# Half of a block's G groups behind its last layer-1 tile, and layer 2 dealt out over three periods, in a fused gather, interaction and tower kernel

## The reference

```
for W in (W0, W1):                       # W0: 39*39 x 128, W1: 39*128 x 128
    xk = einsum('bid,bjd,ijh->bhd', x0, xk, W.reshape(39, Hk, 128))
    outs.append(xk)
z = sum(concatenate(outs, axis=1), axis=-1)          # 512 x 256
h = relu(concatenate([z, dense_ctx]) @ W_top1 + b_top1)   # 272 -> 512
h = relu(h @ W_top2 + b_top2)                             # 512 -> 256
y = h @ W_top3                                            # 256 -> 1
```

## Time and profile before

| | us |
|---|---|
| median of three executions | 284.72 |
| the profiled execution | 284.26 |
| its span on the core | 282.5 |
| PE busy | 228.4 |
| DVE busy | 163.8 |
| ACT busy | 153.4 |
| POOL busy | 136.8 |

### The profile page before, as it was taken

The page is one execution under the profiler, slowest core; times in us unless marked ns, Lnnn a source line. Parts: engine busy times, 40 slices in busy tenths (PEclk is TensorE's granted clock), DMA queues, the critical chain, the costliest instruction groups (busy, mean ns, idle before and its releaser), DMA issues.

```text
span 282.5 us, 4480 instructions
## 1 busy us (share of the span) xinstructions
PE 228.4 (81%) x1548; PEld 190.5 (67%) x1548; DVE 163.8 (58%) x309; ACT 153.4 (54%) x298; POOL 136.8 (48%) x135
## 2 busy tenths in 40 slices
PE   0000349798988999984999999999999999999897
PEld 0000348455767777974977878999687799978696
DVE  6556660398875887535454786674566856542301
ACT  1133133599776897525384786654667857531301
POOL 4787777777777777777777777200000000000000
PEclk9999958669999999996899999999999999999999
DMA  4434640992210111111011012010101010000000
GB/s 78 112 121 123 169 128 9 251 284 33 28 29 10 26 23 21 29 19 19 6 17 22 9 26 31 7 24 3 23 2 17 8 25 9 15 15 12 2 0 0
DMA packets 29862, 12.58 MB, mean 45 GB/s; under 512 B 21438, under 2 KB 27672, under 8 KB 29840
## 3 DMA queue, kind: packets, MB, share of 16 engines
q1 hardware_dynamic: 25648, 11.22, 15.9%
q0 software_dynamic: 4192, 1.08, 4.6%
HBM read 9.66 MB, written 0.00 MB: 34 GB/s over the span
## 4 chain that ended last, share of the span: by engine, by line
PE 46%; POOL 34%; issue 13%; ACT 4%; DMA 2%; ACTq 0%
POOL emb L263 34%; PE turn_bank L340 10%; PE x_bank L305 5%; PE turn_bank L351 4%; PE x_bank L308 4%; PE x_bank L307 4%; PE pair_bank L288 4%; PE misc_bank L277 2%; PE turn_bank L374 2%; PE g_bank L328 2%; PE x_turn_bank L316 2%; PE g_bank L329 2%; PE g_bank L332 2%; ACT x1h L669 1%; ACT prod_hi L656 1%
## 5 line engine op out<-in xcount | busy, mean ns | idle before, releaser
L263 POOL DMA_INDIRECT emb<-tbl,ids_sb x131 | 136.6, 1043 | 42.1 <-issue 39.6
L651 ACT ACTIVATE prod<-pair_bank 128x512 f32<-128x512 f32 (+1 forms) x112 | 66.6, 598 | 46.9 <-PE pair_bank L288 46.9
L305 PE MATMUL x_bank<-prod_hi,pair_w_hi 128*128 128x512 f32 (+1 forms) x112 | 64.8, 579 | 4.5 <-ACT x1h L669 4.5
L531 DVE TENSOR_TENSOR prod_lo<-prod,prod_hi 128x512 fp32r<-128x512 f32 x96 | 62.1, 687 | 2.9
L288 PE MATMUL pair_bank<-x,sel 117*128 117x512 bf16 (+1 forms) x112 | 45.0, 407 | 7.8 <-ACT prod L651 6.2
L340 PE MATMUL turn_bank<-g_sb,w_sb 128*128 128x128 f32 x312 | 42.0, 277 | 0.6 <-ACT g_sb L684 0.6
L340 PEld LDWEIGHTS turn_bank<-g_sb,w_sb 128*128 128x128 f32 x312 | 40.2, 194 | 2.1 <-ACT g_sb L684 0.9
L656 ACT ACTIVATE prod_hi<-prod 128x512 fp32r<-128x512 f32 x64 | 40.3, 630 | 0.0
L308 PE MATMUL x_bank<-prod_hi,pair_w_lo 128*128 128x512 f32 x96 | 38.5, 401 | 0.0
L307 PE MATMUL x_bank<-prod_lo,pair_w_hi 128*128 128x512 f32 x96 | 38.3, 399 | 0.0
L521 DVE CAST prod_hi<-prod 128x512 fp32r<-128x512 f32 x48 | 21.5, 447 | 28.7 <-ACT prod L651 28.2
(11 more groups left out here) (92 smaller groups left out, 278.6 us busy)
## 6 DMA issues: line engine op xcount, KB each, us to landing
xblk<-xs SPq DMA_DIRECT2D x128, 20.0 KB
emb<-tbl,ids_sb POOLq DMA_INDIRECT x131, 2.5
tab<-small SPq DMA_DIRECT2D x2, 625.0 KB
wt<-w_top SPq DMA_DIRECT2D x2, 512.0 KB
small_ids_i<-small_ids SPq DMA_DIRECT2D x2, 500.0 KB
small_ids_i<-small_ids SPq DMA_DIRECT2D x1, 562.5 KB
tab<-small SPq DMA_DIRECT2D x1, 562.5 KB
wa<-pair_w_a SPq DMA_DIRECT2D x1, 448.0 KB, 14.8
```

The source lines that it names most:

```text
L263: pool.indirect_dma_start(out=emb[:, at:at + D], out_offset=None, in_=tables[f], in_offset=bass.IndirectOffsetOnAxis(ap=ids_sb[:, c * M + ...
L305: mm = pe.matmul(x1_bank[:, :], pair_w_hi[p, t, :], prod_hi[p, k % 2, t, :], start=(t == 0), stop=(t == FULL))
L531: dve.tensor_tensor(prod_lo[:, k % 2, t, :] if t < FULL else prod_hi[rows, k % 2, t, :], prod[rows, (NT * k + t) % RING, :], prod_hi[rows, ...
L651: act.activation(prod[0:ROWS[t], n % RING, :], pair_bank[n % 2][0:ROWS[t], :], ACT.Square).then_inc(sq_done, 1)
```

## The change

In each period PE issues groups 0 and 1 of `contract_d` at t = 4 and 5 and groups 2 and 3 behind the loop over t; before, the four stood at t = 3, 4, 5 and 6. The copies of G on ACT and DVE move accordingly. Layer 2 of a chunk, before 21 steps in the period with j = 2 and 18 in the one with j = 3, is dealt out evenly over 21 places in the periods with j = 2, j = 3 and the next j = 0 (13 steps in each), for chunk 2 over 14 places in two periods. The tower, before in the periods with j = 0 (`mlp1`, `mlp2`) and j = 1 (`mlp3`), stands wholly in the one with j = 1, and its last copy, `keep_y`, in the one with j = 2. The tail's code is the same.

```diff
+            def layer2_part(k, t):
+                c, j = k // NB, k % NB
+                at, n = {2: (c - 1, 0), 3: (c - 1, NT), 0: (c - 2, 2 * NT)}.get(j, (-1, 0))
+                steps = 2 * NT if at == NCH - 2 else 3 * NT
+                i0, i1 = ((n + t + e) * M // steps for e in (0, 1))
+                if 0 <= at and n + t < steps and i0 < i1:
+                    layer2(at, i0, i1)
...
@@ PE, period(k), for t in range(NT)
-                    if t >= NT - NG and k >= 2:
-                        contract_d(k - 2, t - (NT - NG))
-                    if j == 2 and c >= 1:
-                        layer2(c - 1, 3 * t, 3 * t + 3)
-                    if j == 3 and c >= 1 and t < 6:
-                        layer2(c - 1, 21 + 3 * t, 24 + 3 * t)
+                    if t in (4, 5) and k >= 2:
+                        contract_d(k - 2, t - 4)
+                    layer2_part(k, t)
...
-                    if j == 0 and c >= 2 and t == 2:
+                    if j == 1 and c >= 2 and t == 1:
                         mlp1(c - 2)
-                    if j == 0 and c >= 2 and t == 6:
+                    if j == 1 and c >= 2 and t == 4:
                         mlp2(c - 2)
-                    if j == 1 and c >= 2 and t == 1:
+                    if j == 1 and c >= 2 and t == 6:
                         mlp3(c - 2)
...
+                if k >= 2:
+                    contract_d(k - 2, 2)
+                    contract_d(k - 2, 3)
@@ DVE, period(k)
-                tiles(k, 4, 6)
-                if j == 0 and c >= 2:
+                if j == 1 and c >= 2:
                     relu1(c - 2)
+                tiles(k, 4, 7)
                 if k >= 2:
                     keep_g(k - 2, 1)
-                tiles(k, 6, NT + 1)
+                tiles(k, 7, NT + LAG)
                 if k >= 2:
                     keep_g(k - 2, 3)
-                tiles(k, NT + 1, NT + LAG)
@@ ACT, period(k)
+                if j == 1 and c >= 2:
+                    keep_z2(c - 2)
                 tiles(k, 0, 1)
                 if k >= 2:
                     keep_x1(k - 2)
...
-                if j == 0 and c >= 2:
-                    keep_z2(c - 2)
+                if j == 2 and c >= 2:
+                    keep_y(c - 2)
+                tiles(k, 1, 5)
+                if k >= 2:
+                    keep_g(k - 2, 0)
+                tiles(k, 5, 6)
...
                 if j == 1 and c >= 2:
                     relu2(c - 2)
-                tiles(k, 1, 4)
-                if k >= 2:
-                    keep_g(k - 2, 0)
-                if j == 1 and c >= 2:
-                    keep_y(c - 2)
-                tiles(k, 4, 6)
...
+                tiles(k, 6, 7)
+                keep_x1h(k - 1)
                 if k >= 2:
                     keep_g(k - 2, 2)
-                tiles(k, 6, 7)
-                keep_x1h(k - 1)
```

More of the change, by code:

```diff
@@ L708, in period @@
                     split_second(c + 1)
-                if j == 0 and c >= 2:
-                    keep_z2(c - 2)
+                if j == 2 and c >= 2:
[4 more added lines that the diff above has]
+                tiles(k, 5, 6)
+                if j == 3 and c + 1 < NCH:
+                    keep_turned(c + 1)
                 if j == 1 and c >= 2:
                     relu2(c - 2)
-                tiles(k, 1, 4)
-                if k >= 2:
-                    keep_g(k - 2, 0)
-                if j == 1 and c >= 2:
-                    keep_y(c - 2)
-                tiles(k, 4, 6)
-                if j == 3 and c + 1 < NCH:
-                    keep_turned(c + 1)
+                tiles(k, 6, 7)
+                keep_x1h(k - 1)
                 if k >= 2:
                     keep_g(k - 2, 2)
-                tiles(k, 6, 7)
-                keep_x1h(k - 1)
                 tiles(k, 7, NT + 1)
```

## The result

The changed kernel takes 287.9 us, median of four executions (287.0 to 289.03), against 284.89 us of the kernel before (283.92 to 285.29): ratio 1.0116, interval 1.0081 to 1.0151, so 3.0 us slower. The forecast was 287.0, with a range of 284.3 to 289.3.

The account below looks back on a forecast made before the run. GpSimd's gathers were taken to bound the kernel until 130.94 us, PE afterwards. Behind that, 2.45 - 3.35 + 2.1 + 1.0 + 0.1 = +2.3 us gave a median of 287.0 us, range 284.3 to 289.3.

Parts of the forecast that it names:

- the restart "at about 131": Sign in the changed profile: PE issues again after waiting for chunk 2's gathered rows at about 131 us, as before (130.94).
- PE's wait "about 10 us": Sign in the changed profile: PE's wait for chunk 2's gathered rows grows from 5.15 to about 10 us.
- A seam at the gather, and nothing gained ahead of it: Up to 130.94 us GpSimd's gathers set the pace, afterwards PE; savings ahead only lengthen PE's wait, 0 us.
- Part 1: Layer 2 dealt out: 11 steps of chunk 0 move behind the gather wait at 0.223 us each, +2.45 us (2.0 to 2.9).
- Part 2: Two groups behind the last tile cover PE's waits for x1h at period starts and tail, -3.35 us (-2.0 to -3.5).
- rival D: Denser period ends: x1h and group 1's copy hold groups 2 and 3, 0.3 in nine periods, +2.7, 289.7 us; chance 0.08.
- Part 3: keep_y behind keep_x1: PE's first layer 2 step waits for y in periods 10 and 14, +2.1 us (1.3 to 2.8).
- rival B: The two new waits, on y and on xs, don't show since ACT and DVE are less behind: 284.4 us; chance 0.15.
- Part 4: DVE's later period end: turn_x waits for xs, about 0.75 us in period 11, 0.25 in 15; +1.0 us (0 to 1.6).
- Rival A: Gathers end earlier, 1.24 us each instead of 1.35, 5 us at most, making the kernel faster: 282.0 us; chance 0.07.
- Rival C: Slow clock behind PE's restart shortens or lengthens from 5.4 us: 285.7 or 288.3 us; chance 0.1 for both together.

Follow-up runs that it names:

- best version: Kernel before, with chunk 0's layer 2 ahead of the gather wait, later chunks' at tiles 1 to 6, mlp3 behind its last tile, keep_y next: 282.9 us, 0.993.

## Why the prediction was right

The direction, the size and the mechanism behind the seam held: 2.3 us were forecast there, 2.55 measured. Two of its signs did not come: the restart "at about 131" was at 134.30 in the profile, and PE's wait "about 10 us" was 7.12. Step by step:

- **A seam at the gather, and nothing gained ahead of it.** Shown: without a seam the same change is worth 0.9996. That the landing stays where it was is not shown: it came 3.36 us later in the one profile, and by what is left over in the medians (below) about 0.5 us typically. This was not forecast, and that it is so small in the median is luck: executions of one kernel differ by 0.3 to 6.7 us here.
- **Part 1, 11 steps moved behind it, +2.45.** Measured +1.6 to +2.0 by putting chunk 0's steps back; the rest of it is a wait of 0.8 that layer 2 hides in period 8.
- **Part 2, x1h, -3.35.** In the changed kernel all these waits are gone; the interval from period 9 to 10 gives 0.64 for one. Its sum is not measured by itself; what is left of 2.55 when 2.45, 2.4 and 0.7 of the other parts are taken off is -3.0. As a statement on the groups by themselves it was wrong: they win nothing without layer 2 or tower in the same period (148.94 against 148.86). The prediction named this reserve under rival D, 3 us against 2.8, and tied it to layer 2 in the period. Behind the seam D's waits didn't come; at the ends of periods 2 to 5, without layer 2, they did (0.34 to 0.48).
- **Part 3, y, +2.1.** Idle 0.93 and 0.92 us, intervals 1.19 us longer each, 2.4 in sum. Only 1.0 of it can be had back by moving `keep_y`, as group 3's copy holds the same step. With these waits rival B is out.
- **Part 4, xs, +1.0.** Idle 0.51 us in period 11, and no wait in period 15. From `turn_x1` of period 11 to that of 12 it takes 15.19 us now, 16.44 before; 5 steps fewer (1.12) and no wait for x1h (0.80) would give 1.92 less, it is 1.25, so 0.7 are lost. Mis-sized, 0.7 instead of 1.0; the prediction's own times, 4.1 and 3.45, already gave 0.65 and not 0.75 for period 11.
- **Rival A** had the sign the wrong way round in this profile. I let spacing between DVE and gathers only help. Of the 3.36 us by which the rows landed later in the profile, 1.4 arose between gathers 12 and 18, where both kernels run the same code (gather 18 starts at 28.69 us, for 27.27). That part is chance as far as the runs show: in the changed kernel's second profile, without a seam, it starts at 26.99. The other 2 us are the size of the higher mean in both kernels with moved groups. In the profiles with such groups the rows were taken between 131.0 and 133.1 us, in the one of before at 129.7, but in that of the best version, whose groups are not moved, at 131.0 too. As only one profile of the kernel before has a seam, it is not settled whether the move or chance made the gathers slower.
- **Rival C**, the slow clock: 2.98 instead of 5.40 us behind the restart, worth 1.2 us in that one execution.

The median difference of 3.0 us is 2.55 behind the seam (to within 0.5) and about 0.5 of gathers and clock, which is what was left over, not measured on its own.

## What to carry to other kernels

Find out up to which moment another queue sets the pace; work that stands ahead of that moment is free there and costs in full behind it, though no engine's total changes. Spreading work evenly is then no virtue in itself: first fill the wait. And a cover moved in front of one wait is only worth something if what it consists of doesn't wait itself; the next copy in line must be looked at before the first one.

## What the runs showed of the hardware

A gather took 943 ns in the mean with VectorE (DVE) idle and 1042 ns in the dense stretch of the kernel before. A remainder, the operation with two SBUF inputs, stood beside each of the twelve long ones there, 1.13 to 1.45 us (the earlier trace rows has the longest); but 14 others that overlapped one by more than 0.3 us stayed at or below 1.1. With a one-input copy in its place the executions spread over 0.3 us (five of them) instead of 2 (eleven). The Trainium skill, GPSIMD Engine Reference, Specifications, says that VectorE instructions with two SBUF inputs contend with GpSimd; these runs agree in direction. They don't show that the second input is the cause, since gathers beside one-input copies took up to 1.28 us too.

The same kernel took 285 us on some chips and 417 to 418 us on two others. There PE issued 16 products between 60 and 100 us, without any wait for data that the profile shows. The cause is open. The main loop ran there at the pace of the other chips (136.14 us from period 8 on, for 136.21).

After PE's wait at the seam the clock was low for 2.98 to 6.83 us, between kernels that run nearly the same code there, and in two of them it fell only 0.7 and 2.3 us behind the restart. At half a microsecond of a busy PE for each, that is up to 1.9 us between two profiles.
